# Cross attention: the first two pairs' probabilities turned between the key projections, and a batch's output projection moved behind the next batch's last values

## What is computed

```python
xn = layer_norm(x, g1, b1)                    # here x is the context: 4 x 4096 x 256
ln_lat = layer_norm(latents, g2, b2)          # here the latents: 4 x 256 x 256
q = ln_lat @ Wq                               # 16 heads of 64
kv = jnp.concatenate([xn, ln_lat], axis=1) @ Wkv
k, v = jnp.split(kv, 2, axis=-1)
weight = jnp.einsum('bhld,bhnd->bhln', q * scale, k * scale)
weight = jnp.where(full_mask[:, None, None, :], weight, neg)
weight = jax.nn.softmax(weight, axis=-1)
out = jnp.einsum('bhln,bhnd->bhld', weight, v)
return out @ Wout                             # added to x
```

## Time and profile before

| | before |
|---|---|
| median of 3 runs | 2299.36 us |
| the profiled execution: its time, its span | 2297.52 us, 2295.7 us |
| cross attention (first score to last product with `wout`) | 53 to 756 us of the span |
| PE busy in 57 to 757 us, granted clock there | 657.25 of 700 us, 0.98 |
| granted clock in 276 to 282 us | 0.72 |
| DVE's second `normalise` of batch 1 | 274.93 us, 1.22 us long |
| last exponential of a steady chunk step; that step's successor begins its keys | 155.01 us, 0.50 us long; 155.07 us |
| DVE, ACT, POOL busy in 57 to 757 us | 459.60, 406.13, 86.92 us |

### The profile page before, as it was taken

How to read it: one execution, slowest core, us unless ns; L and a number is a source line. 1 busy time by engine, 2 the same in 40 slices (tenths; PEclk the granted TensorE clock), 3 DMA queues, 4 the chain that set the end, 5 groups by cost and what they waited for, 6 DMA issues and landing times.

```text
span 2295.7 us, 49701 instructions
## 1 busy us (share of the span) xinstructions
PE 2117.8 (92%) x16354; PEld 1715.7 (75%) x16354; DVE 1706.1 (74%) x4834; ACT 1337.3 (58%) x3908; POOL 494.0 (22%) x274
## 2 busy tenths in 40 slices
PE   3899999999998665899999999999999999999986
PEld 3677777777776444788888888888888888888875
DVE  5777577567564466789888978897889788988872
ACT  1667556556554004567666766676667666766651
POOL 2111111111110002223222322232223222322210
PEclk9999999999999787899999999999999999999998
DMA  3000000000000400002110211021102110111000
GB/s 112 7 10 1 6 11 1 6 11 1 6 24 1 147 0 10 13 13 68 31 49 13 68 33 49 13 68 33 49 13 67 33 49 18 62 31 49 13 13 21
DMA packets 47107, 70.12 MB, mean 31 GB/s; under 512 B 9078, under 2 KB 33828, under 8 KB 46628
## 3 DMA queue, kind: packets, MB, share of 16 engines
q1 hardware_dynamic: 44516, 62.34, 8.8%
q10 hardware_dynamic: 2368, 4.98, 0.6%
HBM read 50.54 MB, written 1.05 MB: 22 GB/s over the span
## 4 chain that ended last, share of the span: by engine, by line
PE 54%; issue 2%; ACT 2%; DVE 1%; DMA 1%; POOL 0%; SPq 0%; DVEq 0%; ACTq 0%; POOLq 0%
PE ps_loc L1539 17%; PE ps_loc L1645 10%; PE ps_loc L1616 7%; PE ps_loc L1655 5%; PE ps_loc L1578 4%; PE ps_loc L1589 4%; PE ps_loc L1605 4%; PE ps_loc L1558 3%; DMA late<-y_all 1%; ACT prob_loc L1786 0%; PE ps_loc L1627 0%; DMA w_raw<-in_ffn_Wqkv_dram 0%; PE ps_loc L1522 0%; ACT L1818 0%; POOL rnorm L2269 0%
## 5 line engine op out<-in xcount | busy, mean ns | idle before, releaser
L2269 POOL TENSOR_TENSOR rnorm<-norm_floor,half_loc 128x32 f32<-128x32 f32 x48 | 302.4, 6300 | 621.2 <-DVE norm_floor L1959 499.1
L1539 PE MATMUL ps_loc<-w_high,xT 128*128 128x512 f32 x1152 | 379.1, 410 | 5.4 <-DVE w_low L1948 3.8
L1786 ACT ACTIVATE prob_loc<-prob_loc,top_loc 128x128 f32<-128x128 f32 x768 | 298.5, 398 | 40.1 <-DVE top_loc L2023 37.3
L1645 PE MATMUL ps_loc<-xnT_loc,w 128*128 128x256 f32 (+1 forms) x1056 | 252.7, 385 | 2.4 <-DVE kT_loc L2089 1.2
L644 ACT ACTIVATE prob<-prob,new_top 128x256 f32<-128x256 f32 x512 | 252.1, 496 | 0.0
L1539 PEld LDWEIGHTS ps_loc<-w_high,xT 128*128 128x128 f32 x1152 | 204.7, 189 | 55.7 <-issue 11.8
L820 DVE CUSTOM_DVE_ANT_0 prob<-ps_cross,bias 128x256 f32<-128x256 f32 x512 | 186.2, 420 | 71.2 <-PE ps_cross L435 57.6
L2023 DVE CUSTOM_DVE_ANT_0 prob_loc<-ps_loc,const,rnorm 128x128 f32<-128x128 f32 x768 | 218.6, 344 | 27.2 <-PE ps_loc L1578 25.5
L1778 ACT ACTIVATE qT_loc<-ps_loc 128x512 f32<-128x512 f32 x96 | 57.3, 597 | 301.2 <-PE ps_loc L1558 301.2
L1539 PE MATMUL ps_loc<-w_low,xT 128*128 128x512 f32 x576 | 228.4, 397 | 0.0
L1645 PEld LDWEIGHTS ps_loc<-xnT_loc,w 128*128 128x128 f32 (+1 forms) x1056 | 191.4, 190 | 28.9 <-DVE kT_loc L2089 2.4
(11 more groups left out here) (184 smaller groups left out, 4265.8 us busy)
## 6 DMA issues: line engine op xcount, KB each, us to landing
w_raw<-in_ffn_Wqkv_dram SPq DMA_DIRECT2D x24, 512.0 KB, 5.4
v_mid<-v_loc SPq DMA_DIRECT2D x48, 256.0 KB, 3.6
w_raw<-in_ffn_Wqkv_dram SPq DMA_DIRECT2D x24, 256.0 KB, 4.0
wo<-in_ffn_Wo_dram SPq DMA_DIRECT2D x24, 256.0 KB, 3.6
w<-in_ffn_W_dram SPq DMA_DIRECT2D x12, 341.0 KB, 3.9
w<-in_ffn_W_dram SPq DMA_DIRECT2D x6, 640.0 KB, 4.8
ctx_raw<-in_ctx_dram SPq DMA_DIRECT2D x12, 256.0 KB, 2.6
w<-in_ffn_W_dram SPq DMA_DIRECT2D x12, 256.0 KB
```

The lines of the kernel that those rows point to most:

```text
L1539: ins = pe.matmul(ps[:, DENSE + j % 2, :], xT[:, px, kk, t * P:(t + 1) * P], wqkv[pw][:, kk, col:col + 512], start=kk == 0 and n == 0, sto ...
L1645: ins = pe.matmul(ps[0:n, DENSE + m % 2, part * T:(part + 1) * T], w1[:, kk, col:col + n], xnT[:, kk, :], start=kk == 0, stop=kk == KD - 1)
L1786: ins = act.activation(pr, pr, ACT.Exp, bias=top[:, h, t:t + 1], scale=-1.0, accum_out=total[:, h, t:t + 1])
L2269: pool.tensor_tensor(rnorm[:, b % 2, t, :], norm2_floor[:, :], half[:, :], ALU.pow).then_inc(rnorm_done, 8)
```

## The change

Three things are moved; no arithmetic changes.

1. In every step, `turn_probs(last, 0)` and `turn_probs(last, 1)` leave `attend` and stand ahead of key groups 2 and 3. `scores(u, 0)` and `scores(u, 1)` follow each other behind the keys; `scores(u, 0)` no longer waits for `k_done`. ACT's order follows: copy pair 0, keys 2, copy pair 1, keys 3, copy pair 2, `copy_parts`, copy pair 3.
2. At a batch's end, `finish` is split into `turn_norm` and `project_out`. `values(u, (2, 3))` stands between the two `turn_norm`, and all products with `wout` (now in banks OUT) behind them. ACT copies the first half ahead of the last pair's exponentials. DVE's `add_x` stands behind `values_out(u, (2, 3))`. The next latents are turned through banks TURN.
3. `project_q` waits for the values but the last two instead of for all. The first step's last values go through banks PROJ.

```diff
@@ PE
             def project_q(u, turn):
                 pe.wait_ge(lat_done, turn)
-                pe.wait_ge(v_done, u)
+                pe.wait_ge(v_done, u - 8)
...
-            def keys(u, src, free):
+            def keys(u, src, free, last=None, turn=1):
+
                 pe.wait_ge(w_split, KD)
                 for j in range(4):
+                    if j == 2 and last is not None:
+                        pe.wait_ge(lat_done, min(turn + 1, B))
+                    if j >= 2 and last is not None:
+                        turn_probs(last, j - 2)
                     if j < 2:
                         free(j)
                     else:
...
             def scores(u, pair, banks=PAIR_SCORE):
-                if pair < 2:
+                if pair == 0:
                     pe.wait_ge(k01_done, u + U)
+                    pe.wait_ge(v_done, u)
+                if pair == 1:
                     pe.wait_ge(k_done, u + U)
-                if pair == 0:
-                    pe.wait_ge(v_done, u)
...
             def attend(u, last, turn):
                 pe.wait_ge(x_done, turn * 2)
-                for g in range(4):
+                scores(u, 0)
+                scores(u, 1)
+                for g in range(1, 4):
...
+            def project_out(u, turn):
+
+                pe.wait_ge(back_done, u)
+                for part in range(2):
+                    for t in range(TT):
+                        pe.wait_ge(fin_done, turn * 4 + 2 * part + t + 1)
...
@@ PE, ahead of the first batch
+            for j in (2, 3):
+                pe.wait_ge(v_done, U + 4 * (j - 1))
+                values(U, (j,), latT_parts[1], FIRST_VALUES)
             pe.wait_ge(s_read, 2 * U)
-            values(U, (2, 3), latT_parts[1])
-            turn_lat(2, OUT)
+            pe.wait_ge(inT_done, pe.snap(uc_reg))
+            turn_lat(2, TURN)
+            pe.wait_ge(v_done, 2 * U)
...
@@ PE, change(turn)
                 pe.wait_ge(v_done, u + 8)
-                finish(turn, 0)
-                finish(turn, 1)
-                pe.wait_ge(x_done, turn * 2 + 2)
+                turn_norm(turn, 0)
                 values(u, (2, 3), latT_parts[(turn + 1) % 2])
+                turn_norm(turn, 1)
+                project_out(u, turn)
...
@@ ACT, attend
                 for pair in range(4, PAIRS):
+                    if uc is None and pair == PAIRS - 1:
+                        act.wait_ge(back_full, u)
+                        finish(turn, 0)
                     exps(u, pair)
+                if uc is None:
+                    finish(turn, 1)
...
@@ DVE, change(turn)
                 input_next(u, bits > 0)
+                values_out(u, (2, 3))
                 add_x(turn)
-                values_out(u, (2, 3))
```

More of the change, by code:

```diff
@@ L276, in cross_attention @@
         PAIR_SCORE, FIRST_SCORE = (SCORE, PROJ), (SCORE, OUT)
-        VALUES = (PROJ, PROJ + 1, SCORE, SCORE + 1)
+        VALUES, FIRST_VALUES = (PROJ, PROJ + 1, SCORE, SCORE + 1), (PROJ, PROJ + 1, PROJ, PROJ + 1)
         sem = k.sem
@@ L437, in scores, with values @@
                 ins.then_inc(s_full, 2)
-            def values(u, js, src):
+            def values(u, js, src, banks=VALUES):
                 for j in js:
@@ L445, in values @@
                         for kk in range(KD):
-                            ins = pe.matmul(ps[:, VALUES[j], :], src[:, x, kk, t * P:(t + 1) * P],
+                            ins = pe.matmul(ps[:, banks[j], :], src[:, x, kk, t * P:(t + 1) * P],
                                             wkv[:, w, kk, INNER + part * 512:INNER + (part + 1) * 512],
@@ L502, in attend, with turn_norm @@
                     turn_probs(last, 2 * g + 1)
-                    if g:
-                        weigh(last, g - 1, turn)
+                    weigh(last, g - 1, turn)
                 weigh(last, 3, turn)
-            def finish(turn, part):
+            def turn_norm(turn, part):
                 pe.wait_ge(fin_ready, turn * 2 + part + 1)
@@ L515, in finish @@
                     ins.then_inc(fin_full, 1)
[L516 to L522, removed]
+            def project_out(u, turn):
[3 more added lines that the diff above has]
+                        pe.wait_ge(fin_done, turn * 4 + 2 * part + t + 1)
+                        for pair in range(4 * part, 4 * part + 4):
+                            ins = pe.matmul(ps[:, OUT + t, 0:D], oT[:, pair, t * P:(t + 1) * P], wout[:, pair, :],
+                                            start=pair == 0, stop=pair == PAIRS - 1)
+                        if part:
+                            ins.then_inc(x_full, 1)
             turn_lat(1, SCORE)
@@ L550, in step @@
                     uc = pe.snap(uc_reg)
-                    chunk_keys(u, uc)
+                    chunk_keys(u, uc, last, turn)
                     attend(u, last, turn)
@@ L565, in change @@
                 project_q(u, turn + 1)
-                lat_keys(u, turn + 1)
+                lat_keys(u, turn + 1, last)
                 attend(u, last, turn)
@@ L595, in _ @@
             pe.wait_ge(v_done, pe.snap(u_reg))
-            finish(B, 0)
+            turn_norm(B, 0)
             back(last, 1)
-            finish(B, 1)
+            turn_norm(B, 1)
+            project_out(pe.snap(u_reg), B)
         @block.scalar
@@ L620, in queries_out, with keys_out @@
                                    ACT.Copy, scale=-float(DH) ** -0.5).then_inc(q_done, 1)
-            def keys_out(u):
+            def keys_out(u, j):
                 act.wait_ge(s_full, u)
[L624 to L627, removed]
+                act.wait_ge(k_full, u + 4 * (j + 1))
+                act.activation(kT[:, 2 * j:2 * j + 2, :], ps[:, PROJ + j % 2, :].rearrange("p (i n) -> p i n", i=2),
+                               ACT.Copy).then_inc(k_done, U // 2)
             def copy_parts(u, uc):
@@ L659, in output_out, with attend @@
                     .then_inc(oT_done, 4)
-            def attend(u, last, turn):
-                for pair in range(ON_ACT):
-                    probs_out(last, pair)
+            def attend(u, last, turn, uc=None):
+                probs_out(last, 0)
+                keys_out(u, 2)
+                probs_out(last, 1)
+                keys_out(u, 3)
+                probs_out(last, 2)
+                if uc is not None:
+                    copy_parts(u, uc)
+                probs_out(last, 3)
                 act.wait_ge(x_full, turn * 2)
@@ L695, in step @@
                     u, last = act.snap(u_reg), act.snap(act.snap(u_reg) - U)
[L696 to L698 removed]
+                    attend(u, last, turn, act.snap(uc_reg))
                     act.reg_add(u_reg, u_reg, U)
@@ L834, in running, with values_out @@
                 ch.link(dve.tensor_copy(top[:, :, heads], new_top[:, :, heads]))
-            def values_out(u, js):
+            def values_out(u, js, banks=VALUES):
                 dve.wait_ge(o_full, u)
@@ L840, in values_out @@
                     dve.wait_ge(v_full, u + 4 * (j + 1))
-                    dve.tensor_copy(v[:, t, part * 512:(part + 1) * 512], ps[:, VALUES[j], :]).then_inc(v_done, U // 4)
+                    dve.tensor_copy(v[:, t, part * 512:(part + 1) * 512], ps[:, banks[j], :]).then_inc(v_done, U // 4)
             def probs_out(u, pair):
@@ L894, in add_x @@
                     xt = k.x[:, (turn - 1) * TT + t, :]
-                    dve.tensor_tensor(xt, ps[:, SCORE + t, 0:D], xt, ALU.add).then_inc(x_done, 1)
+                    dve.tensor_tensor(xt, ps[:, OUT + t, 0:D], xt, ALU.add).then_inc(x_done, 1)
             lat_out(chain, 1, SCORE)
@@ L917, in _ @@
             running(ch, U, 1)
-            values_out(U, (2, 3))
-            lat_out(ch, 2, OUT)
+            values_out(U, (2, 3), FIRST_VALUES)
+            lat_out(ch, 2, TURN)
             done(ch)
@@ L971, in change @@
                 input_next(u, bits > 0)
+                values_out(u, (2, 3))
                 add_x(turn)
-                values_out(u, (2, 3))
                 if turn + 2 <= B:
-                    lat_out(ch, turn + 2, OUT)
+                    lat_out(ch, turn + 2, TURN)
                 done(ch)
```

23 lines of the change are left out of this document (8 added, 15 removed).

## The result

The changed kernel takes 2274.03 us, the median of 5 runs (2269.11 to 2275.18), against 2299.36 (2296.36 to 2299.97): a ratio of 0.989, with a 95% interval of 0.9877 to 0.9902. It is 25 us or 1.1% faster. Run again, beside other runs of before, the two gave 2273.25 (2269.25 to 2274.98) and 2299.43, 0.9884 (0.9865 to 0.9904).

The account below looks back on a forecast made before the run. PE, busy 92% of the span, was taken to bound the kernel, with only its idle time to win. Terms summed to -21.8 us on 2297.5, giving 2275.7; plus 1.8 for the median, 2277 was said, range 2270 to 2283.

Parts of the forecast that it names:

- next batch's keys, to pair 4's transposes: Keys behind a batch's end: 0.6 us of waiting instead of 1.7 in two batches, -0.4 in the third; -2.6 us.
- The steady step: 11 chunk steps: 0.32 us wait at pair 2's transposes goes, 0.32 comes at pair 3's scores, 0.06 a restart; +0.7 us.
- S: The start of `scores(u, 0)` in a chunk step, from which the forecast counts its waits.
- The first step: First chunk step: last values start in banks PROJ without the 1.72 us wait; -3.5 us, ends -2.2 and -3.7.
- The batch's end: First turned half to next keys: 12.4 us without PE idling or clock loss, saving 4.9, 3.4 and 4.9; -13.2 us.
- The queries: Ahead of the queries: 0.94 us copy wait goes but loop exits remain; 0.7 us won in batch 1, -0.9 in all.
- The tail: After the last batch: `back` and products start earlier, ending at 753.7 against 756.1; -2.3 us, between -4.0 and -0.6.
- plus 1.7 for one stretch at the low clock: Tail: 1.7 us added to the products' 2 x 3.56 us for one low-clock stretch.
- No other wait came at the batch's end: Rival, 15%: ACT or DVE later, one 2.3 us wait with 1.7 clock loss stays in two or three batches; 2287.
- `scores(u, 1)` and `scores(u, 2)` show no bracket: Rival, 12%: steady step gets longer, these scores having 0.1 and 0.08 us of room; 0.4 us in 15 steps, 2283.
- ACT never held PE at the keys: Rival "Slower", 3%: late exponentials on ACT make PE stand at the keys in all 15 steps; 4 us would give 2337.
- The exits are free: Rival, 12%: queries start where the values end, the last 2.3 us of their waits go too; 2275.

Follow-up runs that it names:

- batch_end_only: Changed kernel with pairs 0 and 1 turned behind the keys again, the rest as changed: 2276.68 us, 0.9903 of before.
- interleave_only: Kernel before plus only the transposes of pairs 0 and 1 between key groups, with ACT's order and split keys wait: 2291.65 us, 0.9967 of before.
- act_half_last: Changed kernel with ACT's copy of the first turned half back behind all exponentials: 2272.98 us in one execution.
- queries_wait_all: Changed kernel with the queries waiting for all values again: 2270.28 us in one execution.
- loop_groups_of_8: Changed kernel with the chunk loops in 2 groups of 8 instead of 4 of 4: 2286.61 us in one execution.
- pair3_later: Changed kernel with pair 3's transposes ahead of pair 3's scores instead of behind them: 2268.39 us, 0.9875 of before.

## Why the prediction was right

The forecast was 2277 us, and 2274.03 was measured. Between the same rows of the two profiled executions:

| term | forecast | measured | read from |
|---|---|---|---|
| up to pair 4's transposes of the first chunk step | -3.5 | -3.3 | 95.97 before, 92.65 changed |
| 11 steady steps | +0.7 | -0.9 | 37.45, 37.37 |
| first turned half to next keys, 3 batches | -13.2 | -15.0 | 17.33, 15.75, 17.00; 11.87, 11.87, 11.33 |
| next batch's keys, to pair 4's transposes | -2.6 | -2.6 | batch 1: 17.69, 16.61; third group waits 0.55 and 0.56 |
| queries | -0.9 | -1.0 | last values to queries in batch 1: 3.99, 3.07 |
| tail | -2.3 | -0.8 | 40.3, 39.5 |
| sum | -21.8 | -23.6 | spans: -23.5 |

- **The steady step: the mechanism right, a size off.** The new bracket stood where it was put, 4.24 us behind S. "0.32 us go and 0.32 come" left out two sizes. The two sets of transposes between keys take 0.79 us each, together 0.4 less than behind the keys, and the keys cut in three take 0.26 more. The wait that went was worth 0.38 (the transposes behind it also got shorter by 0.06), and `scores(u, 2)` and `scores(u, 3)`, apart and behind a wait, take 2.36 us and not 1.93. In sum the step is 0.08 shorter instead of 0.06 longer. Why the transposes are shorter there is open.
- **The first step: right by luck, from two errors.** The values ran in 3.75 us from 70.03, so they ended 0.7 us sooner than taken. Most of that comes of 0.8 us which I had not counted: the very first scores no longer wait for ACT's last keys (52.52 for 53.29; in `batch_end_only`, which has that wait again, the bracket of 1.08 us is back). The entry into the loop behind `v_done` took from 74.65, where DVE's copy ends, to 76.94, 2.3 us and not 1.0. And 1.5 of the 3.3 us are a low clock that lasted longer in the execution before (5.28 us for the values against 3.75), which `interleave_only` shows to come and go.
- **The batch's end: right, and 0.6 us a batch too small.** I had taken 7.12 us for the products and 1.02 for each turned half; in one unbroken stretch they took 6.90, 0.85 and 0.87. `batch_end_only` and `act_half_last` show that PE's order carries this term. Of the 15.0 us 3.2 are the low clock of batches 1 and 3, which the wait brought in 3 of 6 cases.
- **The queries: right in the mechanism.** The way out of the loops, not the copy, holds PE in batches 2 and 3: shown by `queries_wait_all` and `loop_groups_of_8`. Batch 1 gave 0.9 us where 0.7 was forecast. By 0.86 us a number two fewer leave 0.2 of the 1.91 us, and not the 0.4 that I took; PE showed no bracket. The estimate of 0.16 us for a number passed over, which the prediction made from the 108 and 51 ns of the Trainium skill, Advanced Engine Details and Errata, section Control Flow Timing, did not hold here: 0.95 us. The rival built on it fell.
- **The tail: "plus 1.7 for one stretch at the low clock" failed in this execution.** The granted clock of 716 to 726 us was 0.55. The low level began in the first turned half and held through `back`, the second turned half and part of the products. The three sets of eight transposes took 1.10, 1.9 and 1.76 us, where 0.9 to 1.0 is usual, and the products 8.7 for 6.9. That is some 3.8 us, 2.1 more than forecast, and nearly all of the 2.1 lies ahead of the products, where I had put none. The kernel before lost 3.4 us in its tail (5.41 and 5.39 us against 3.72), with other work between the same two waits. So it is not shown that the waits' standing closer is the cause. The seven executions with this order give 37.5 to 39.5 us; the forecast, 37.9, lies among them. What the runs show is that the low clock's place and length vary, and that filling the second wait pays.
- **The rivals.** No other wait came at the batch's end; `scores(u, 1)` and `scores(u, 2)` show no bracket; ACT never held PE at the keys. "The exits are free" had 2275, nearer to the measured time than my own 2277, and is wrong: the time alone would not have told the two apart, the brackets do.
- **The sum.** It came within 2 us partly by luck: the steady step and the batches' ends gave 1.6 and 1.8 us more than forecast, the tail 1.5 less.

The medians differ by 25.3 us, the profiled executions by 23.5; the spread of the changed kernel's runs, some 6 us, is larger than any term but the batches' ends. Not all of it arises in the part that was changed: from the linear attention's first transposes to the first of the next block took 127.7 us in both profiled executions above (767.65 to 895.38, 744.12 to 871.80) and 123.2 in `queries_wait_all` (744.27 to 867.48), with the same code there and a granted clock of 0.82, 0.83 and 0.86.

## What to carry to other kernels

Put independent work of the bottleneck engine into its waits at the stage boundaries first: here one move of 2.9 us of matmuls within each batch's end gave 15.0 of the 23.5 us between the profiled executions, 3.2 of them clock, while moving work inside the steady step traded one wait for another of nearly the same size, until `pair3_later` took that away too. When a wait is removed, ask what it was hiding; here a loop's exit took its place, and the profile kept the old name for it. Give the low clock a range and not a number in a forecast: here the same tail took 37.5 to 39.5 us.

## What was not expected of the hardware

- Each chunk number or empty group passed over on PE's way out of the nested chunk loops cost 0.95 us, over eight exits, beyond some 2.9 us that do not show; entering the loop with a word to load cost 2.3 us where PE had waited for DVE just ahead of it.
- The same 2.30 us of idling was followed by a lower clock in 3 of 6 batch ends (5.31, 5.35 and 5.41 us for 16 instructions against 3.72), differently placed in two kernels with the same wait. Without the wait it was so in none of 30.
- With the same order of PE's work and the same two waits (2.75 and some 2.5 to 2.7 us) the tail took 37.5 to 39.5 us in seven executions.
- Eight 128x128 transposes took 0.79 us from start to start with keys behind them and 0.97 to 1.02 with scores, or products with the values, behind them.
